# A graph network with an expert layer on one core: in the last node update, transposes and logits one step later, and the second bias added by VectorE

## The reference

```
hidden = relu(layer_norm(hidden + m, g, b))
```

```
adjustment = relu(hidden @ W1.T + b1) @ W2.T + b2     # 256 -> 256 -> 256
x1   = x + xn + adjustment                            # xn: the normalized input
z    = layer_norm(x1)                                 # twice, the second for the experts
logits = z @ Wr + br                                  # 8 experts, top 2 per token
out  = x1 + sum of the two experts' outputs, weighted
```

## Time and profile before

| | us |
|---|---|
| median of 3 runs | 3940.0 |
| lowest and highest | 3938.81, 3954.16 |
| the profiled execution's own time | 3954.87 |
| its span | 3953.1 |
| `uf_phase` in it, first L1501 to last L1568 | 3270.6 to 3488.3 |

### The profile page before, as it was taken

The page is one execution under the profiler, slowest core; times in us unless marked ns, Lnnn a source line. Parts: engine busy times, 40 slices in busy tenths (PEclk is TensorE's granted clock), DMA queues, the critical chain, the costliest instruction groups (busy, mean ns, idle before and its releaser), DMA issues.

```text
span 3953.1 us, 102089 instructions
## 1 busy us (share of the span) xinstructions
PE 3440.6 (87%) x32589; PEld 2682.7 (68%) x32590; DVE 2614.5 (66%) x6732; ACT 2183.1 (55%) x6515; POOL 2492.7 (63%) x2501
## 2 busy tenths in 40 slices
PE   6887968888888898888889888888888888859998
PEld 3444657777777657777777755777777766659998
DVE  7887368887888646888788854888788884341111
ACT  4998855555555355555555535555555551224443
POOL 3776067777777427777777724777777772224444
PEclk9998989999999899999999989999999996769999
DMA  2000345555550035555554014555555203236664
GB/s 73 1 1 7 130 134 147 164 149 149 147 148 17 22 130 160 153 155 149 150 150 120 0 56 134 149 164 149 148 145 155 78 1 106 87 121 180 185 181 121
DMA packets 231294, 456.26 MB, mean 115 GB/s; under 512 B 90096, under 2 KB 134013, under 8 KB 222863
## 3 DMA queue, kind: packets, MB, share of 16 engines
q0 software_dynamic: 161376, 322.67, 30.9%
q1 hardware_dynamic: 69822, 132.43, 10.0%
HBM read 562.97 MB, written 47.19 MB: 154 GB/s over the span
## 4 chain that ended last, share of the span: by engine, by line
issue 27%; PE 27%; POOL 18%; DMA 9%; DVE 3%; POOLq 2%; ACT 1%; DVEq 0%; ACTq 0%
POOL arena L529 17%; DMA arena<-kv_d,gidx 8%; PE bank L1657 5%; PE bank L1669 5%; PE bank L1467 2%; PE bank L1501 2%; PE bank L1428 2%; PE bank L1444 2%; PE bank L1502 1%; PE bank L1457 1%; PE bank L1422 1%; PE bank L1549 1%; PE bank L1561 1%; POOLq L529 1%; POOL gidx L522 1%
## 5 line engine op out<-in xcount | busy, mean ns | idle before, releaser
L529 POOL DMA_INDIRECT arena<-kv_d,gidx x1764 | 1889.7, 1071 | 519.6 <-issue 481.2
L1227 ACT ACTIVATE kt_s<-bank 128x512 f32<-128x512 f32 x882 | 526.0, 596 | 823.9 <-PE bank L1444 821.2
L1457 PEld LDWEIGHTS bank<-qbd,kt_s 128*128 128x128 f32 x7056 | 937.8, 193 | 27.2 <-ACT kt_s L1227 3.4
L1444 PE MATMUL bank<-ident,arena 128*128 128x128 f32 x3528 | 683.5, 285 | 298.2 <-DMA arena<-kv_d,gidx 280.3
L1457 PE MATMUL bank<-qbd,kt_s 128*128 128x128 f32 x7056 | 932.8, 275 | 2.6 <-ACT kt_s L1227 2.6
L771 DVE TENSOR_REDUCE sc<-bank 128x32 f32<-128x512 f32 x882 | 610.2, 692 | 213.4 <-PE bank L1457 186.3
L1444 PEld LDWEIGHTS bank<-ident,arena 128*128 128x128 f32 x3528 | 403.2, 142 | 465.1 <-DMA arena<-kv_d,gidx 444.6
L797 DVE TENSOR_TENSOR att<-at_s,arena 128x512 f32<-128x512 f32 x882 | 612.9, 695 | 57.3 <-DVE at_s L790 36.5
L1467 PE MATMUL bank<-att,arena 128*64 128x64 f32 x14112 | 610.3, 229 | 19.7 <-DVE arena L814 19.7
L1467 PEld LDWEIGHTS bank<-att,arena 128*64 128x64 f32 x14112 | 488.5, 138 | 167.1 <-issue 150.6
L814 DVE TENSOR_TENSOR arena<-bank,arena 64x64 f32 x1764 | 393.5, 223 | 221.6 <-DVE arena L814 109.2
(11 more groups left out here) (239 smaller groups left out, 3969.6 us busy)
## 6 DMA issues: line engine op xcount, KB each, us to landing
arena<-in_pack SPq DMA_DIRECT2D x56, 1030.0 KB, 5.1
arena<-kv_d,gidx POOLq DMA_INDIRECT x1764
kv_d<-arena SPq DMA_DIRECT2D x50, 256.0 KB, 2.0
xin<-hid_d SPq DMA_DIRECT2D x75, 128.0 KB, 2.0
arena<-in_w SPq DMA_DIRECT2D x8, 1024.0 KB, 5.3
kv_d<-arena SPq DMA_DIRECT2D x5, 1280.0 KB, 5.3
hid_d<-arena SPq DMA_DIRECT2D x50, 128.0 KB, 2.0
rec_d<-arena POOLq DMA_INDIRECT x241
```

Source lines behind the costliest of these rows:

```text
L529: pool.indirect_dma_start(kv[:, t // UB, t % UB, :], None, kv_d, bass.IndirectOffsetOnAxis(gidx[:, h, t - h * HT:t - h * HT + 1], 0), boun ...
L1227: act.activation(kt_s[:, p % 2], bank[3 + p % 2][:, :].rearrange("p (u c n) -> p u c n", u=2, n=P), ACT.Copy).then_inc(S.kT_ready, 1)
L1444: ins = pe.transpose(bank[3 + p % 2][:, o:o + P], kv[:, t // UB, t % UB, c * P:(c + 1) * P], ident[:, :])
L1457: ins = mm(bk[:, o:o + P], kt_s[:, p % 2, u, c, :], qbd[:, p % 4, u, :], start=False, stop=(c == KC - 1), skip_group_check=True)
```

## The change

Three things change in `uf_phase`:

- TensorE's transposes of z and logits come one step later: tile k-10 and tile k-11 are taken in step k, and its loop has one step more. ScalarE's copy out of bank 6 takes tile k-10, and its loop has one step more too.
- The matmul of ones with the second bias (L1547) is gone; the product with W2 starts the sum.
- VectorE adds the second bias to the token's row in place, in step k for tile k-5, between the scaling of tile k-1 and x1 of tile k-6. A new semaphore, `f_xo`, tells that it is done.

In the input phase one semaphore (`std_ready`) is folded into another (`chain_in`). The diff, cut to its core:

```diff
@@ vector, uf_phase
                     if 1 <= k <= NT:
                         scaled(l, k - 1)
+                    if 5 <= k < NT + 5:
+                        n = k - 5
+                        if n == 0:
+                            dve.wait_ge(S.wl_landed, all_landed)
+                        dve.wait_ge(x_w1_landed[n % G], (n // G + 1) * 16)
+                        dve.tensor_tensor(xo[:, n % G, :], xo[:, n % G, :], bf2, ALU.add).then_inc(S.f_xo, 1)
                     if 6 <= k < NT + 6:
                         n = k - 6
                         dve.wait_ge(S.f_adj_done, n + 1)
-                        dve.wait_ge(x_w1_landed[n % G], (n // G + 1) * 16)
+                        dve.wait_ge(S.f_xo, n + 1)
...
@@ vector, input_phase
-                dve.wait_ge(S.std_ready, 1)
+                dve.wait_ge(S.chain_in, 2 * NT + 1)
                 dve.reciprocal(rs0, sd0).then_inc(S.chain_in, 1)
-                dve.wait_ge(S.chain_in, 2 * NT + 1)
+                dve.wait_ge(S.chain_in, 2 * NT + 2)
...
@@ scalar
-            act.activation(sd0, mv0[:, :, 1], ACT.Sqrt, bias=epsc[:, 0:1]).then_inc(S.std_ready, 1)
+            act.activation(sd0, mv0[:, :, 1], ACT.Sqrt, bias=epsc[:, 0:1]).then_inc(S.chain_in, 1)
...
@@ scalar, uf_phase
-                for k in range(NT + 9):
+                for k in range(NT + 10):
...
-                    if k >= 9:
-                        n = k - 9
+                    if k >= 10:
+                        n = k - 10
                         act.wait_ge(S.f_zT_done, n + 1)
...
@@ tensor, uf_phase
-                for k in range(NT + 10):
+                for k in range(NT + 11):
                     if 3 <= k < NT + 3:
                         hidden_turned(l, k - 3)
-                    if 9 <= k < NT + 9:
-                        n = k - 9
+                    if 10 <= k < NT + 10:
+                        n = k - 10
                         pe.wait_ge(S.f_z, n + 1)
                         if n:
                             pe.wait_ge(S.f_zT_ready, n)
...
-                        mm(bank[3 + n % 3][:, D:2 * D], onesrow[:, :], bf2[0:1, :], start=True, stop=False, skip_group_check=True)
                         for c in range(KC):
                             ins = mm(bank[3 + n % 3][:, D:2 * D], rT[:, n % G, c, :], wf2[:, c, :],
-                                     start=False, stop=(c == KC - 1), skip_group_check=True)
+                                     start=(c == 0), stop=(c == KC - 1), skip_group_check=True)
...
-                    if k >= 10:
-                        n = k - 10
+                    if k >= 11:
+                        n = k - 11
                         pe.wait_ge(S.f_zT_ready, n + 1)
```

More of the change, by code:

```diff
@@ L309, in build @@
                  "scattered oht_done oht_copied cnt_done cnt_copied chain_s chain_r "
-                 "chain_in std_ready x0_ready shift_ready xb_ready xT_done xT_ready proj_done hout_ready "
+                 "chain_in x0_ready shift_ready xb_ready xT_done xT_ready proj_done hout_ready "
                  "wl_landed bias_ready hT_done hT_ready q_done q_ready kvp_done kvp_ready ee_done ee_ready sums_zeroed "
@@ L313, in build @@
                  "agg_done edges_all u_turned u_done u_sum u_stat u_mean u_root u_rs "
-                 "f_u_done f_r_ready f_adj_done f_x1 f_stat f_mean f_root f_rs f_z f_xn f_zT_done "
+                 "f_u_done f_r_ready f_adj_done f_xo f_x1 f_stat f_mean f_root f_rs f_z f_xn f_zT_done "
                  "f_zT_ready f_lg_done f_lg_ready r_exp r_exped chain_x r_occ r_rank r_slots w2_landed r_eid "
```

## The result

| | before | after |
|---|---|---|
| median, us | 3945.4 (4 runs) | 3882.9 (4 runs) |
| lowest, highest | 3938.8, 3954.2 | 3878.6, 3886.2 |
| ratio | | 0.984, interval 0.982 to 0.987 |
| span of the profiled execution | 3953.1 | 3880.2 |

In the new code the moved lines are L1507/L1508 (update, before L1501/L1502), L1513 (hidden row, before L1507), L1548 (transposes of z, before L1542), L1554 (product with W2, before L1549), L1566 (with W1), L1573 (logits); on VectorE L943 is the new add, L950 makes x1, L962 the mean, L974 z; on ScalarE L1301 and L1302 are the two roots and L1309 the copy.

A forecast was written before the change was run, and what follows sets the result against it. TensorE was taken to bound uf_phase, 8.75 us a step, through a small gap and a lowered clock. 26.4 + 3.0 + 3.5 - 1.2 = 31.7 us off the median 3940.0 gave 3908.3, range 3887 to 3926.

The forecast's parts named there:

- The gap: TensorE's wait before z's transposes in 17 middle steps: stays through ScalarE's copy, shrinking 0.12 us, from 1.14 to 1.02.
- The sign that I gave for it: Profile after: TensorE's wait ahead of the transposes put down to ScalarE's copy in 17 steps, 1.0 us each.
- The bias matmul: L1547 on TensorE's chain, 21.9 us in 25 steps; 0.91 us a step in the 17 middle ones.
- The first four steps: Start of uf_phase: without L1547's pieces, one of 1.15 us and three of 0.62, they gain 3.0 us.
- The clock: TensorE's granted clock in 17 middle steps: mostly short falls, one step in ten without; 8.75 to 7.2 us, 26.4 gained.
- The low end of the range: Fastest time allowed, 3887 us: steps of 5.97 us, 47.3 + 5.3 = 52.6 us gained.
- If the clock no longer falls: Bound for the 17 middle steps: 5.97 us each, from 6.71 less 0.62 and 0.12.
- The end: End of uf_phase: 3.5 us gained in the last four steps, 1.2 us lost behind the last L1549.
- The last four steps: Late in uf_phase: without L1547's pieces, two of 0.62 us and two of 1.15, they gain 3.5 us.
- The extra pair of transposes and logits: TensorE's added work behind the last L1549, pieces of 0.57 and 0.65 us: costs 1.2 us.
- The add: VectorE's bias add, 0.45 us 25 times, 11 us: costed at nothing, hidden by VectorE's wait for the update.
- The page's rule: TensorE's clock falls only behind longer idle gaps, so it stays full and a step gains 0.74 us; sum didn't use it.

The follow-up runs named there:

- e4_copy_ahead: Changed kernel with ScalarE's copy out of bank 6 put ahead of the two roots; 92.9 us under the kernel before, ratio 0.976.
- e1_bias_only: Kernel before with the bias matmul replaced by VectorE's add, transposes and logits not moved; 50.4 us under the kernel before, ratio 0.987.
- e3_full_row_bias: Kernel before with the one-row bias matmul made a full one, identity times bias on 128 partitions; 44.2 us under the kernel before, ratio 0.987.
- e2_late_only: Kernel before with transposes, copy and logits one step later, bias matmul kept; 4.3 us under the kernel before, ratio 0.9988.
- e5_ahead_bias_kept: Kernel before with later transposes and logits, ScalarE's copy ahead of the roots, one-row bias matmul kept; 67.5 us under its before, ratio 0.984.
- e10_longer_gap: Changed kernel with a third, unused root on ScalarE ahead of the copy; 40.3 us under its kernel before, ratio 0.991.
- e8_add_twice: Changed kernel with VectorE's bias add made twice in each step; 61.2 us under its kernel before, ratio 0.985.

## Why the prediction was wrong

- **The gap.** Right, as to its place and its cause: it stayed, since the copy out of bank 6 was moved along with the transposes and closed the loop in z's stead; e4_copy_ahead shows it. It was mis-sized slightly: I let the gap shrink by 0.12 us, the distance of the two ends, and it shrank by 0.03 (1.14 to 1.11), as TensorE starts 0.15 us behind ScalarE's copy and 0.06 behind VectorE's z. And it stands in 15 steps, not 17, since the transposes begin a step later and the first tile's wait for no copy. The sign that I gave for it, waits put down to ScalarE's copy, appeared in none of the 15: the profile names z in all of them, wrongly.
- **The bias matmul.** It was priced at 0.62 us at full clock, its own piece of the chain. Its true price is 0.82, as the steps without a gap show (4.43 to 3.61): the product with W2 became shorter too. Its piece of the chain at full clock was 1.06 us and is 0.86 now, and the idle time ahead of its weight loads went from 16.1 to 1.8 us (the group of the kernel before, over 3265 to 3492, below; the other stands above). The chain had put these 0.2 us under L1549. The first four steps gave 5.6 us and not 3.0: 4 x 0.82 = 3.3 is the product, 1.4 are the gap and the transposes of the first tile, which come a step later now, and the rest is a longer stretch at half clock in the first step of the kernel before.

```profile
L1549 PEld LDWEIGHTS bank<-arena 128*128 128x128 f32 x100 | 26.0, 287 | 16.1 <-issue 12.5
```

- **The clock.** This is the step that failed. I wrote that the clock should be back sooner, and let it fall still in nine steps of ten: 7.2 us a step. It fell in three of fifteen, and the mean of the 17 steps is 5.64 us (95.9 / 17), which gives 52.8 us in place of 26.4. I had seen that the falls come behind the gap and asked only what brings the clock back. I did not ask what lowers it, and whether the gap still does so without the one-row product. With the gap kept, taking the product out moves the clock from 0.70 to 0.82 (e1_bias_only), and making it a full one to 0.87 (e3_full_row_bias). The later transposes, which I had counted for 0.12 us a step, leave it at 0.70 beside the product (e2_late_only) and bring it to 0.94 without. Without the gap the product does no harm to it (e5_ahead_bias_kept).
- **The low end of the range.** "If the clock no longer falls" was 5.97 us, 3887. The step of 6.71 us from which it came had its transposes at half clock (0.69 us where 0.41 is the piece at full clock in the changed kernel), and 0.2 us of the bias matmul's price was missing. The real step is 5.58. With it the low end would have been 3881, and the result just inside.
- **The end.** The last four steps were to give 3.5 us; the last three alone gave 6.6 (17.5 to 10.8). In the kernel before two of them ran partly at half clock (6.1 and 7.0 us where 4.4 is one at full clock), and now none does. The extra pair of transposes and logits was to cost 1.2 us. From the last product with W2 to the last logits it is 7.8 us against 8.6: TensorE ran these at full clock and waited for VectorE and ScalarE between them. No cost was seen.
- **The add.** Right: 419 ns, hidden, and hidden still when doubled. VectorE's wait for the update, its cover, is 2.1 us a time (43.9 / 21) and not the 3.5 that I had expected, as the steps are shorter.
- **The page's rule.** By "TensorE: Matmul & The Clock Gate" of the Trainium skill, section "Why this matters for your kernels", gaps this short would not lower the clock. The kernel before disagrees with 0.70. The changed one comes near it with 0.94, but e10_longer_gap, with 1.3 us and without L1547, is at 0.83 and disagrees again.

What stays open is why the clock falls just in some of the equal steps of the changed kernel. The falls are regular: they begin at 3333.3, 3357.2 and 3381.1, 23.9 us apart both times. In e8_add_twice, whose TensorE work is the same, there are five, and the last four of them are again 23.9 us apart. So they don't look like chance, and how many fall into so few steps may hang on where the first one comes, which no run tests. Open is also why the bias-only kernel, whose gap is longer by 0.03 us only, has the clock at 0.82 where the changed one has 0.94; 12 us lie between the two.

## What to carry to other kernels

Price a gap on TensorE twice: by its length, and by what it does to the clock; beside a one-row product the second was nearly twice the first here (35 and 20 us). Products on few rows (a bias by a row of ones) cost about double a full one here and, beside a gap, went with a lower clock, so move them to an idle engine or make them full. When a wait is moved by software pipelining, list every semaphore that the waiting instruction has, and move all of their producers; here one instruction of ScalarE, put two places earlier, gave 30 us more than the change.

## What was not expected of the hardware

- A float32 product on one row or on 32 costs a step 0.82 us (two instructions of 256 columns, full clock), on 128 rows 0.43.
- The granted clock over the steps with a gap of 1.1 us: 0.70 with a one-row product, 0.80 with 32 rows, 0.87 with 128, 0.82 with none; and with none and the later transposes 0.94.
- 0.2 us of gap more took the clock from 0.94 to 0.83, while 0.2 us less left it about where it was (0.96).
